# One scan of 448 columns in place of two of 224, in a state-space layer that runs beside DMA gathers

## The chip, the cores and the metric

The kernel runs on one core of a Trainium2 chip. The metric is the time of one execution on the device in microseconds. All times in the text are in us unless marked ns.

## What is computed

Four layers on eight images of 56 x 56 pixels with 128 channels. Layers 0, 2 and 3 are deformable convolutions with a feed-forward part behind them: for each pixel and each of 4 groups, 9 points with learned offsets are sampled from a table, weighted and added. Layer 1 is a state-space block (the scan), and this is its core:

```python
def step(h, t):
    dt_t, u_t, B_t, C_t = t
    h = h * jnp.exp(dt_t[..., None] * A) + (dt_t * u_t)[..., None] * B_t[:, :, None, :]
    y = jnp.einsum('bkdn,bkn->bkd', h, C_t)
    return (h, y)
ts = (dt.transpose(3, 0, 1, 2), xs.transpose(3, 0, 1, 2), Bsm.transpose(3, 0, 1, 2), Csm.transpose(3, 0, 1, 2))
h0 = jnp.zeros((B, K, Di, N), dtype=x.dtype)
_, ys = jax.lax.scan(step, h0, ts)
```

There are K = 4 directions over the image (by rows, by columns, and each of them backward), Di = 256 channels, N = 16 states and 3,136 pixels.

## The kernel before

**Work.** 24 stages (three convolution layers times eight images) follow one another; the state-space layer of each image runs beside them. In a stage, 24 tiles of 128 pixels and one of 64 are gathered: GpSimd issues one indirect DMA (L761) for every sampling point, 882 a stage, 21,168 in all, each of which reads its 128 indices from SBUF (`d_idx`). Twelve of them (six at the end of a stage) fill one of five buffers `d_g`. VectorE multiplies a buffer by its weights (L1369, "weigh"; the weights come from SBUF, or, where ScalarE has copied them, from PSUM, `l_pm`), PE adds it up through the identity (L1052, "sum"), and only then may GpSimd fill it again: it waits for the semaphore `accq` of the use five buffers earlier. Before every fourth tile it also waits for `idx`, the indices that VectorE computes in L1564.

**The scan.** The 256 channels are two halves of 128 partitions. An image is cut into 7 pieces of 448 pixels, times 4 directions, times 16 states: 448 steps an image, 3,584 in all. Step S needs for each half h the decay exp(dt*A) (ScalarE, L812), the product dt*u*B (VectorE, L1339, both halves in one instruction of 2 x 448 columns into the buffer `hb`, with B spread over the partitions by PE into the bank `l_pb`, L1003), the scan h = decay*h + product along the 448 pixels, in place in `hb`, and the product with C (VectorE, L1349, with C in the bank `l_pc`), which PE adds over the 16 states into `l_acc` (L1034). ScalarE saves the last column of both halves in `l_carry` (L793), from which the next piece's scan of that state begins.

The decay of half 0 lies in PSUM (`dA0`, a part of `l_pm`, one buffer), that of half 1 in SBUF (`dA1`, three buffers, shown as `l_wk`). `hb` has four buffers in SBUF, shown as `l_wk` too.

**Order.** A planner written in Python (class `Planner`) lays out one list of items for all engines before anything runs: ticks of the scan ("s", with PE's "sB" ahead of each), the weighing and summing of the gathers, and the pieces of the convolution, among them. Each engine walks through the list and issues its part of each item, with semaphores in between. The list doesn't depend on how long the instructions take. In a tick, VectorE's program (function `vector_program`) issues for step S: the scan of half 0 (L1326, 448 columns, semaphore `sh`), the first 224 columns of half 1 (L1328, semaphore `s1h`), the dt*u*B product of step S+1 (L1339, semaphore `f_pb`), after a wait for `s1h` (L1342) the other 224 columns of half 1 (L1343, semaphore `sh`), which start from the last column of the first part, and the C product of step S-1 (L1349, semaphore `f_pc`, with a wait for the carry, `ca`, L1348). For the directions 2 and 3 all goes backward along the columns.

**Who waits for a scan.** ScalarE's decay of half 0 for step S+1 waits for the scan of half 0 of step S (L809), since they share one buffer; its decay of half 1 for the step three later, and the carry (L792), wait for both halves. PE's spread of B for step S+2 waits for the product of step S+1 (`f_pb`), and its spread of C for the C product before it (`f_pc`).

Of the kernel before, what the change touches and what calls it, by code (L numbers as in the profile page):

```python
# [10 lines left out]
ALU = mybir.AluOpType  # L11
# [27 lines left out]
NSTEP = 16 * len(PIECES)  # L39
# [1224 lines left out]
def vector_program(e, J):  # L1264
    m, s = J.m, J.s
# [29 lines left out]
    for item in J.plan:  # L1295
        kind = item[0]
        if kind == "s":
            _, i, sig = item
            S = NSTEP * i + sig
            if sig >= 18 and sig % 16 == 2:  # L1300
                j = sig // 16 - 1
                P = 28 * i + j
                kd, c = PIECES[j]
# [11 lines left out]
            if 0 <= sig < NSTEP:  # L1315
                kd, c = PIECES[sig // 16]
                n = sig % 16
                hb, dA1 = m.hb[S % 4], m.dA1[S % 3]
                ini = [0.0 if c == (6 if kd >= 2 else 0) else m.carry[:, h, n:n + 1] for h in range(2)]

                way, one, two, mid = slice(None), slice(0, 224), slice(224, 448), 223
                if kd >= 2:
                    way, one, two, mid = slice(None, None, -1), slice(447, 223, -1), slice(223, None, -1), 224
                e.wait_ge(s["f_pb"], J.free("B", S))
                e.wait_ge(s["dA0"], S + 1)
                e.tensor_tensor_scan(hb[:, 0, way], m.dA0[:, way], hb[:, 0, way], ini[0], ALU.mult, ALU.add).then_inc(s["sh"], 1)  # L1326
                e.wait_ge(s["dA1"], S + 1)
                e.tensor_tensor_scan(hb[:, 1, one], dA1[:, one], hb[:, 1, one], ini[1], ALU.mult, ALU.add).then_inc(s["s1h"], 1)  # L1328
            if sig + 1 < NSTEP:
                x = S + 1  # L1330
                P, n = divmod(x, 16)
# [2 lines left out]
                if sig == -1:  # L1334
                    e.wait_ge(s["p_pc"], J.full("pi2", 7 * i + 6))
                    for b, v_ in enumerate(both(7 * i + 6)):
# [1 line left out]
                e.wait_ge(s["p_pb"], J.full("B", x))  # L1338
                e.tensor_tensor(m.hb[x % 4][:, :, :], m.dtu[P % 2][:, :, :], bc(m.pb[:, 0:448], 1, 2),  # L1339
                                ALU.mult).then_inc(s["f_pb"], 1)  # L1340
            if 0 <= sig < NSTEP:
                e.wait_ge(s["s1h"], S + 1)  # L1342
                e.tensor_tensor_scan(hb[:, 1, two], dA1[:, two], hb[:, 1, two], hb[:, 1, mid:mid + 1],  # L1343
                                     ALU.mult, ALU.add).then_inc(s["sh"], 1)
            if 1 <= sig <= NSTEP:
                x = S - 1
                e.wait_ge(s["p_pc"], J.full("C", x))
# [23 lines left out]
        elif kind == "h":  # L1371
            _, i, j, st = item
            P = 28 * i + j
            kd, c = PIECES[j]
# [148 lines left out]
        elif kind == "pr":  # L1523
# [11 lines left out]
            two = lambda x: x.rearrange("p t (j a) -> p t j a", a=2)  # L1535
# [54 lines left out]
        elif kind == "ch":  # L1590
# [45 lines left out]
PLAIN = ("c_w l_w da xi0 xi1 tab0 tab1 hdo dg htc xr0 xr1 xo0 xo1 vx0 vx1 xn0 xn1 z0 z1 vr0 vr1 vo0 vo1 "  # L1636
         "p_r0 p_r1 p_pm p_pb p_pc f_r0 f_r1 f_pm f_pb f_pc f_a0 f_a1 pa aexp cst dv "
         "weighed accq ysa ytp yta idx wtr w0 pv py exd bst agg sqd x1r xor gbr dgr bsq bnr "
         "wps dA0 dA1 s1h sh ca accd d1 d2 hd0 md m2 lo ab ex uu qq s1 ln pag psq xir brd lag lsq xmr gsq gt gb tg").split()


def program(nc, a, out, n_img=8, layers=(0, 1, 2, 3)):
    with ExitStack() as ctx:
        ctx.enter_context(nc.allow_non_contiguous_dma("weights and constants, once a stage"))

        def sb(name, shape, dt=F32):
            return ctx.enter_context(nc.sbuf_tensor(name, shape, dt))

        def ps(name, shape):
            return ctx.enter_context(nc.psum_tensor(name, shape, F32))  # L1650

        def dram(name, shape):
            return nc.dram_tensor(name, shape, F32, kind="Internal").ap()

        sems = {n: ctx.enter_context(nc.semaphore("s_" + n)) for n in list(PLAIN) + GSEMS}
        nums = sorted(sems[n].num for n in PLAIN)
        assert nums == list(range(nums[0], nums[-1] + 1))
        order, plan = schedule(n_img)
        J = Job(n_img, order, plan, Mem(sb, ps, dram, n_img), sems, a, out)
        with nc.Block() as block:  # L1660
            block.sync(lambda e: sync_program(e, J))
            block.gpsimd(lambda e: gpsimd_program(e, J))
            block.scalar(lambda e: scalar_program(e, J))
            block.vector(lambda e: vector_program(e, J))
            block.tensor(lambda e: tensor_program(e, J))
        totals = gather_totals(J)
        for q in range(0, len(totals), 10):
            part = totals[q:q + 10]
            nc.gpsimd.inc_swdge_sem([sems[g] for g, _ in part], [x for _, x in part], mode="sub")
        nc.all_engine_barrier(sems_to_clear=range(nums[0], nums[-1] + 1))  # L1670
# [75 lines left out]
```

## Time and profile before

| | |
|---|---|
| median of 3 runs | 29,863.57 us (29,856.42 to 29,863.9) |
| profiled execution, its time | 29,810.02 us |
| its span in the trace | 29,808.1 us |
| granted TensorE clock, mean | 0.848 of full speed |
| busy: PE | 22,658.6 us (76% of the span) |
| busy: VectorE | 22,829.2 us (77%) |
| busy: ScalarE | 12,217.9 us (41%) |
| busy: GpSimd | 21,878.7 us (73%) |
| mean DMA rate | 62 GB/s |

Engines are named PE (matmul), PEld (its weight loads), DVE (VectorE), ACT (ScalarE), POOL (GpSimd) and SP in the rows. In a group of instructions, `x` is the count, then come the busy time in us and the mean of one in ns, then the idle time of the engine just before them in us and what ended most of it. In the list of waits the columns are: who waited for whom, us in total, times, the longest. "issue" is time in which the engine waited for nothing that the profile shows; issuing itself doesn't count as busy, so GpSimd's 73% leaves out the time between two gathers. In a timeline the first number is the start in us, the second the duration in us, and the brackets hold the idle time of the engine before it, where there is any. Instructions of VectorE overlap a little in the records: the next one starts before the one ahead has written its last column.

### The profile page before, as it was taken

How to read it: one execution, taken by the hardware profiler on the slowest of the kernel's cores; microseconds unless marked ns; L12 is line 12 of the kernel's file. 1: busy time of each engine (PE TensorE's matmuls, PEld its weight loads, DVE VectorE, ACT ScalarE, POOL GpSimd, SP SyncE). 2: the span in 40 equal slices, each digit the busy share in tenths (PEclk: the TensorE clock that was granted, in tenths of full speed). 3: DMA queues.
4: the chain of work that ended last, by engine and by line, in shares of the span. 5: the costliest groups of instructions: out<-in, count | busy, mean ns of one | idle time of the engine just before them, and what ended most of it. 6: DMA issues, size and time to landing. Idle time of an engine off the chain costs nothing.

```text
span 29808.1 us, 287351 instructions
## 1 busy us (share of the span) xinstructions
PE 22658.6 (76%) x94224; PEld 14342.0 (48%) x94224; DVE 22829.2 (77%) x36118; ACT 12217.9 (41%) x21747; POOL 21878.7 (73%) x21172
## 2 busy tenths in 40 slices
PE   5588788787877888777878788777877787777444
PEld 4444455454544455444544454445544454445433
DVE  2398988989689879897799959986899869884212
ACT  1144444444444445444444444444444444443000
POOL 5777777777677777777677767776677767576767
PEclk7798888888888889888888888888988888887666
DMA  3212122221221222212222122212222121112221
GB/s 77 70 58 68 52 76 64 60 68 54 72 62 57 65 70 64 64 54 66 62 65 68 52 74 58 61 54 70 62 60 62 56 72 54 47 50 68 63 58 53
DMA packets 2410662, 1854.55 MB, mean 62 GB/s; under 512 B 1686546, under 2 KB 2045508, under 8 KB 2409164
## 3 DMA queue, kind: packets, MB, share of 16 engines
q0 software_dynamic: 677376, 1388.62, 15.4%
q1 hardware_dynamic: 1731788, 447.55, 6.7%
q8 instruction: 745, 12.21, 0.2%
q14 instruction: 753, 6.17, 0.1%
HBM read 1569.35 MB, written 265.21 MB: 62 GB/s over the span
## 4 chain that ended last, share of the span: by engine, by line
DVE 32%; PE 28%; POOL 17%; issue 13%; ACT 6%; DMA 1%; SPq 1%; DVEq 0%; ACTq 0%; POOLq 0%
POOL d_g L761 17%; DVE l_wk L1349 7%; DVE l_wk L1326 6%; PE d_p L1052 6%; PE l_acc L1034 5%; DVE l_wk L1343 5%; DVE d_g L1369 4%; PE d_pr L1200 3%; DVE l_wk L1328 2%; PE d_pr L1254 2%; ACT l_pm L812 2%; PE d_pr L1087 2%; PE d_pr L1066 1%; ACT L988 1%; PE d_pr L1247 1%
## 5 line engine op out<-in xcount | busy, mean ns | idle before, releaser
L761 POOL DMA_INDIRECT d_g<-table,d_idx x21168 | 21878.5, 1034 | 7886.6 <-issue 6402.6
L1034 PE MATMUL l_acc<-l_wk,c_ident 128*128 128x448 f32 x14336 | 7285.4, 638 | 384.9 <-DVE l_yx L1314 298.5
L1052 PE MATMUL d_p<-d_g,c_ident 128*128 128x128 f32 x43200 | 6013.0, 303 | 1955.5 <-DVE d_g L1369 1952.8
L1052 PEld LDWEIGHTS d_p<-d_g,c_ident 128*128 128x128 f32 x43200 | 5877.4, 218 | 3015.6 <-DVE d_g L1369 2067.6
L1339 DVE TENSOR_TENSOR l_wk<-l_wk,l_pb 128x896 f32<-128x896 f32 x3584 | 3816.9, 1065 | 1581.6 <-PE l_pb L1003 1577.0
L812 ACT ACTIVATE l_pm<-l_wk,l_a 128x448 f32<-128x448 f32 x3584 | 2270.9, 634 | 6219.4 <-DVE l_wk L1326 6203.8
L1034 PEld LDWEIGHTS l_acc<-l_wk,c_ident 128*128 128x128 f32 x14336 | 3171.3, 223 | 2453.9 <-issue 2276.4
L1349 DVE TENSOR_TENSOR l_wk<-l_wk,l_pc 128x896 f32<-128x896 f32 x3584 | 3795.7, 1059 | 20.7 <-ACT l_carry L793 16.5
L1326 DVE TENSOR_TENSOR_SCAN l_wk<-l_pm,l_carry,l_wk 128x448 f32<-128x448 f32 x3072 | 3498.6, 1139 | 4.9 <-ACT l_pm L812 2.6
L1369 DVE TENSOR_TENSOR d_g<-d_g,d_wt 128x512 f32<-128x512 f32 (+1 forms) x1248 | 798.0, 692 | 2204.3 <-DMA d_g<-table,d_idx 2204.1
L1343 DVE TENSOR_TENSOR_SCAN l_wk<-l_wk 128x224 f32<-128x224 f32 x3584 | 2422.1, 676 | 0.3
L1369 DVE TENSOR_TENSOR d_g<-d_g,l_pm 128x1536 f32<-128x1536 f32 (+1 forms) x1358 | 2350.0, 1730 | 60.5 <-DMA d_g<-table,d_idx 43.9
L812 ACT ACTIVATE l_wk<-l_wk,l_a 128x448 f32<-128x448 f32 x3584 | 2359.4, 659 | 15.1 <-DVE l_wk L1401 0.9
L1003 PE MATMUL l_pc<-l_spl,c_sel 96*128 96x448 bf16 x3584 | 1420.9, 396 | 1141.9 <-DVE l_wk L1349 1137.3
L1328 DVE TENSOR_TENSOR_SCAN l_wk<-l_wk,l_carry 128x224 f32<-128x224 f32 x3072 | 2017.5, 657 | 0.0
L1003 PE MATMUL l_pb<-l_spl,c_sel 96*128 96x448 bf16 x3584 | 1402.8, 391 | 634.1 <-DVE l_wk L1339 632.2
L793 ACT ACTIVATE l_carry<-l_wk 128x2 f32<-128x2 f32 x3584 | 722.8, 202 | 2593.9 <-DVE l_wk L1343 2588.3
L812 ACT ACT_TABLE_LOAD x1193 | 1530.6, 1283 | 20.9
L1200 PE MATMUL d_pr<-d_xt,d_diag 128*128 128x448 f32 x3024 | 1369.9, 597 | 34.1 <-ACT d_xt L927 27.1
L1003 PEld LDWEIGHTS l_pc<-l_spl,c_sel 96*128 96x128 bf16 x3584 | 369.8, 103 | 1836.7 <-DVE l_wk L1349 1677.1
L1254 PE MATMUL d_pr<-d_fc,d_ht 128*128 128x128 f32 (+1 forms) x4800 | 869.3, 337 | 502.3 <-ACT d_ht L988 502.1
L1247 PE MATMUL d_pr<-d_yt,d_fc 128*128 128x256 f32 (+1 forms) x2496 | 749.5, 428 | 540.3 <-ACT d_ht L988 454.3
(180 smaller groups left out, 23375.1 us busy)
## 6 DMA issues: line engine op xcount, KB each, us to landing
d_g<-table,d_idx POOLq DMA_INDIRECT x21168
table<-d_pst SPq DMA_DIRECT2D x2376, 64.0 KB
hd<-d_hst SPq DMA_DIRECT2D x168, 224.0 KB
d_htc<-hd SPq DMA_DIRECT2D x144, 256.0 KB
d_xin<-mid SPq DMA_DIRECT2D x112, 224.0 KB, 3.1
mid<-d_xo SPq DMA_DIRECT2D x192, 128.0 KB, 1.9
d_xres<-mid SPq DMA_DIRECT2D x192, 128.0 KB, 2.1
d_xin<-in_x SPq DMA_DIRECT2D x56, 224.0 KB, 3.4
```

Source lines behind the costliest of these rows:

```text
L761: e.indirect_dma_start(out=m.g[Q % SLOTS][:, j, :], out_offset=None, in_=m.table[k % 2], in_offset=bass.IndirectOffsetOnAxis(ap=m.idx[G % ...
L812: e.activation(m.dA0 if h == 0 else m.dA1[x % 3], m.dt[P % 2][:, h, :], ACT.Exp, scale=m.aa[:, kd, h, n:n + 1]).then_inc(s[f"dA{h}"], 1)
L1003: return e.matmul(bank[:, 0:448], m.sel[:, row + n:row + n + 1].to_broadcast([96, 128]), m.spl[P % 2][:, :], start=True, stop=True)
L1034: ins = e.matmul(m.acc[:, h, 0:448], m.ident[:, :], m.hb[x % 4][:, h, :], start=(n == 0), stop=(n == 15))
L1052: ins = e.matmul(m.p0[:, t % 2 * 128:t % 2 * 128 + 32 * w], m.ident[:, :], m.g[Q % SLOTS][:, w * p:w * p + w, 32 * r:32 * r + 32], start=( ...
L1200: ins = e.matmul(m.r[1][:, 0:448], m.diag[:, j, :], m.xt[:, 8 * c + dy:8 * c + dy + 8, dx:dx + 56], start=(j == 0), stop=(j == 8))
L1326: e.tensor_tensor_scan(hb[:, 0, way], m.dA0[:, way], hb[:, 0, way], ini[0], ALU.mult, ALU.add).then_inc(s["sh"], 1)
L1328: e.tensor_tensor_scan(hb[:, 1, one], dA1[:, one], hb[:, 1, one], ini[1], ALU.mult, ALU.add).then_inc(s["s1h"], 1)
L1339: e.tensor_tensor(m.hb[x % 4][:, :, :], m.dtu[P % 2][:, :, :], bc(m.pb[:, 0:448], 1, 2), ALU.mult).then_inc(s["f_pb"], 1)
L1343: e.tensor_tensor_scan(hb[:, 1, two], dA1[:, two], hb[:, 1, two], hb[:, 1, mid:mid + 1], ALU.mult, ALU.add).then_inc(s["sh"], 1)
L1349: e.tensor_tensor(m.hb[x % 4][:, :, :], m.hb[x % 4][:, :, :], bc(m.pc[:, 0:448], 1, 2), ALU.mult).then_inc(s["f_pc"], 1)
L1369: ins = e.tensor_tensor(g, g, wt, ALU.mult)
```

## The change

The scan of half 1 becomes one instruction of 448 columns, directly behind the scan of half 0 and ahead of the dt*u*B product of the next step; it starts from the carry, as its first part did. The second part, the wait for `s1h` and that semaphore are gone. Nothing else is changed; `sh` still counts two for each step.

```diff
-                way, one, two, mid = slice(None), slice(0, 224), slice(224, 448), 223
-                if kd >= 2:
-                    way, one, two, mid = slice(None, None, -1), slice(447, 223, -1), slice(223, None, -1), 224
+                way = slice(None, None, -1 if kd >= 2 else None)
                 e.wait_ge(s["f_pb"], J.free("B", S))
                 e.wait_ge(s["dA0"], S + 1)
                 e.tensor_tensor_scan(hb[:, 0, way], m.dA0[:, way], hb[:, 0, way], ini[0], ALU.mult, ALU.add).then_inc(s["sh"], 1)
                 e.wait_ge(s["dA1"], S + 1)
-                e.tensor_tensor_scan(hb[:, 1, one], dA1[:, one], hb[:, 1, one], ini[1], ALU.mult, ALU.add).then_inc(s["s1h"], 1)
+                e.tensor_tensor_scan(hb[:, 1, way], dA1[:, way], hb[:, 1, way], ini[1], ALU.mult, ALU.add).then_inc(s["sh"], 1)
...
                 e.tensor_tensor(m.hb[x % 4][:, :, :], m.dtu[P % 2][:, :, :], bc(m.pb[:, 0:448], 1, 2),
                                 ALU.mult).then_inc(s["f_pb"], 1)
-            if 0 <= sig < NSTEP:
-                e.wait_ge(s["s1h"], S + 1)
-                e.tensor_tensor_scan(hb[:, 1, two], dA1[:, two], hb[:, 1, two], hb[:, 1, mid:mid + 1],
-                                     ALU.mult, ALU.add).then_inc(s["sh"], 1)
```

## Rows read from the trace of the kernel before

**Rows 1.** List of waits, whole span: waiter, releaser: us, times, longest

```profile
POOL d_g L761 <- DVE d_idx L1564: 886.6, 11, 303.7
POOL d_g L761 <- PE d_p L1052: 597.5, 148, 34.3
...
DVE l_wk L1339 <- PE l_pb L1003: 1577.0, 739, 10.8
```

**Rows 2.** The gathers: their group, then duration ns min/median/max, first and last start

```profile
L761 POOL DMA_INDIRECT d_g<-table,d_idx x21168 | 21878.5, 1034 | 7886.6 <-issue 6402.6
...
L761 POOL DMA_INDIRECT d_g<-table,d_idx x21168: 938/944/3096, 159.3 to 29764.6; - x200
```

**Rows 3.** Groups, stretch 27,449 to 28,554 us (first), then 2,454 to 3,642 us

```profile
L761 POOL DMA_INDIRECT d_g<-table,d_idx x882 | 836.7, 949 | 359.5 <-issue 268.5 <-DVE d_idx L1564 91.0
...
L761 POOL DMA_INDIRECT d_g<-table,d_idx x882 | 919.9, 1043 | 268.8 <-issue 268.5 <-PE d_p L1052 0.3
...
L1343 DVE TENSOR_TENSOR_SCAN l_wk<-l_wk 128x224 f32<-128x224 f32 x186 | 125.7, 676 | 0.0
```

**Rows 4.** Waits: DVE, 1,400 to 13,406 us (first); POOL, 1,395 to 27,029 us

```profile
DVE d_g L1369 <- DMA d_g<-table,d_idx: 40.1, 15, 8.0
...
POOL d_g L761 <- PE d_p L1052: 573.8, 145, 34.3
POOL d_g L761 <- DVE d_idx L1564: 530.7, 8, 303.7
```

**Rows 5.** Timeline of DVE and POOL from 12,019 us

```profile
12019.36 0.68 DVE L1343 TENSOR_TENSOR_SCAN l_wk<-l_wk 128x224 f32<-128x224 f32 x1
12019.53 1.26 POOL L761 DMA_INDIRECT d_g<-table,d_idx  x1 [0.30 <-issue]
...
12021.10 1.12 DVE L1326 TENSOR_TENSOR_SCAN l_wk<-l_pm,l_carry,l_wk 128x448 f32<-128x448 f32 x1
12021.10 0.94 POOL L761 DMA_INDIRECT d_g<-table,d_idx  x1 [0.30 <-issue]
...
12022.13 0.66 DVE L1328 TENSOR_TENSOR_SCAN l_wk<-l_wk,l_carry 128x224 f32<-128x224 f32 x1
12022.34 1.20 POOL L761 DMA_INDIRECT d_g<-table,d_idx  x1 [0.30 <-issue]
```

**Rows 6.** Timeline of DVE and POOL from 12,069 us

```profile
12069.69 1.81 DVE L1407 TENSOR_TENSOR l_wk<-l_wk,l_xb 128x896 f32<-128x896 f32 x1
12069.99 2.33 POOL L761 DMA_INDIRECT d_g<-table,d_idx  x1 [0.30 <-issue]
```

**Rows 7.** Timeline of DVE alone, one tick without other work

```profile
11999.58 0.65 DVE L1328 TENSOR_TENSOR_SCAN l_wk<-l_wk,l_carry 128x224 f32<-128x224 f32 x1
12000.15 1.05 DVE L1339 TENSOR_TENSOR l_wk<-l_wk,l_pb 128x896 f32<-128x896 f32 x1
12001.13 0.67 DVE L1343 TENSOR_TENSOR_SCAN l_wk<-l_wk 128x224 f32<-128x224 f32 x1
12001.73 1.05 DVE L1349 TENSOR_TENSOR l_wk<-l_wk,l_pc 128x896 f32<-128x896 f32 x1
12002.71 1.13 DVE L1326 TENSOR_TENSOR_SCAN l_wk<-l_pm,l_carry,l_wk 128x448 f32<-128x448 f32 x1
12003.77 0.65 DVE L1328 TENSOR_TENSOR_SCAN l_wk<-l_wk,l_carry 128x224 f32<-128x224 f32 x1
```

**Rows 8.** Lines L1328 and L1343: duration ns min/median/max, first and last start

```profile
L1328 DVE TENSOR_TENSOR_SCAN l_wk<-l_wk,l_carry x3072: 647/657/697, 1494.6 to 27028.2; 128x224 f32<-128x224 f32 x192
...
L1343 DVE TENSOR_TENSOR_SCAN l_wk<-l_wk x3584: 666/676/743, 1399.0 to 27028.9; 128x224 f32<-128x224 f32 x200
```

**Rows 9.** Costliest groups of the page: second half scan, B spread

```profile
L1343 DVE TENSOR_TENSOR_SCAN l_wk<-l_wk 128x224 f32<-128x224 f32 x3584 | 2422.1, 676 | 0.3
...
L1003 PE MATMUL l_pb<-l_spl,c_sel 96*128 96x448 bf16 x3584 | 1402.8, 391 | 634.1 <-DVE l_wk L1339 632.2
```

**Rows 10.** Timeline of POOL at the start of a stage

```profile
3671.72 0.94 POOL L761 DMA_INDIRECT d_g<-table,d_idx  x1 [29.21 <-DVE d_idx L1564]
```

More of the change, by code:

```diff
@@ L1638 @@
          "weighed accq ysa ytp yta idx wtr w0 pv py exd bst agg sqd x1r xor gbr dgr bsq bnr "
-         "wps dA0 dA1 s1h sh ca accd d1 d2 hd0 md m2 lo ab ex uu qq s1 ln pag psq xir brd lag lsq xmr gsq gt gb tg").split()
+         "wps dA0 dA1 sh ca accd d1 d2 hd0 md m2 lo ab ex uu qq s1 ln pag psq xir brd lag lsq xmr gsq gt gb tg").split()
 def program(nc, a, out, n_img=8, layers=(0, 1, 2, 3)):
```

## The prediction, on record before the result was known

> **What bounds the kernel now.** I began with the page's busy times of the engines. PE, VectorE and GpSimd lie close together and none is near the whole span, so the shares name no bound. The list of waits does [rows 1]: in a span of 29,808 us GpSimd waits 886.6 us for the indices and 597.5 us for PE to give a gather buffer back, and for nothing else. The rest of its time is gathers, 21,168 of them at a mean of 1,034 ns, with 6,402.6 us of its own issue between them, 0.30 us each [rows 2]. 21.88 + 6.40 + 0.89 + 0.60 ms is 29.77 of 29.81 ms: the chain of gathers is the span, and nothing can be gained that doesn't shorten it.
>
> Next: what sets the length of a gather. Its median is 944 ns, its shortest 938, its longest 3,096 [rows 2]. The difference of mean and median, 90 ns, times 21,168 is 1.9 ms of stall inside gathers. In a stage without scans (27,449 to 28,554 us) the mean is 949 ns, in one of the same 882 gathers with 186 scan steps (2,454 to 3,642 us) 1,043 ns [rows 3]. So the stall comes with the scan steps: 94 ns x 882 = 83 us a stage.
>
> VectorE doesn't wait for gathers there: in the first half of the stretch with scans it waited 40.1 us for them, while over the whole stretch GpSimd waited 573.8 us for buffers and 530.7 us for indices [rows 4], 303.7 of this in one wait [rows 1]. Gathers, and the VectorE and PE work interleaved with them, go at nearly one pace, with the five buffers between.
>
> **What stalls a gather.** In the timeline [rows 5] the gather begun at 12,019.53 took 1.26 us. The second half scan (L1343) ran until 12,020.04 and the gather ended at 12,020.79, 0.75 us behind it. The gather of 12,022.34 took 1.20 us, and ended 0.75 us after the first half scan (L1328) had. Between them the scan L1326, whose decay lies in PSUM, covered a whole gather, which took 0.94. A gather thus needs something about 0.19 us after its start (0.94 - 0.75), and where a VectorE instruction with both operands in SBUF is running then, it waits for the end of that instruction. A long one holds it to its end too: the product L1407, 1.81 us, stretched a gather to 2.33 us, which ended 0.82 us behind it [rows 6].
>
> The Trainium skill ("SBUF — State Buffer", section "SBUF: two separate sides") has this as a lock on a port pair that the two engines share, held for the whole instruction, by VectorE also with two SBUF inputs against a GpSimd operation that reads SBUF. It speaks against the change, which makes one long hold of two short ones. By the same rule the scans should wait for gathers as well; in the trace they don't.
>
> **The parts, priced.**
>
> 1. VectorE time. In a tick without other work [rows 7] the starts are 0.57 us apart from L1328 to the next instruction, 0.60 from L1343 to the next, 1.06 for the PSUM scan of 448 columns, and 4.19 us from one L1328 to the next. The trace has no SBUF scan of 448 columns. From above its price is the sum of the two, 1.17 us (no gain); from below it is 1.00, the PSUM scan's 1.06 less twice the 0.03 by which the two half scans differ, the only spread of scans in these rows. I take 1.04, near the PSUM scan of the same length. So each step saves 0.13 us, 3,584 steps [rows 8] 0.47 ms of VectorE time. It isn't on the chain of gathers, so it counts only as below.
>
> 2. The wait removed, L1342, costs 0.3 us of idle time before all L1343 together [rows 9]: nothing. What covered it, the product, now stands behind the scan. The product of step S+1 comes about 0.47 us later in the tick, and PE gets the bank of B so much later; behind it PE waits for the C product anyway, 0.98 us later in the tick, which is longer than the B matmul, 0.39 us [rows 9]. Nothing, and if that cover were gone 0.47 us a step at most, on PE. In the other direction the 1,577.0 us in which the product waited for B [rows 1] shrink, since a whole scan comes first. ScalarE's carry is released about 1.1 us earlier in the tick; VectorE needs it only in the next tick.
>
> 3. Gather stalls. A gather comes to this point once in 0.94 + 0.30 = 1.25 us. If an instruction that holds it, of length L, falls there at a random phase, it is hit with chance L/1.25 and costs L/2 on the mean: L x L/2.5 us. Two half scans: (0.57² + 0.60²)/2.5 = 0.274 us a step. A control: 186 steps of it are 51 of the 83 us found above, and the rest is left for the other SBUF operations (L1407 and its neighbours), which is plausible. One scan of 1.04: 0.433 us. The difference is +0.159 us a step, x 3,584 = **+0.57 ms**. Lower bound: in ticks without other work the phases lock. After a stalled gather the next ones ask 1.25, 2.49 and 3.74 us after the scan's end, the next scan runs from 3.04 to 4.08, so each costs 0.34 us: 1.22 ms against 0.98, +0.24 ms. Upper bound: all 1.9 ms of stall belongs to the scans and grows by 0.433/0.274 = 1.58: +1.1 ms. I take +0.57: most steps are longer than the clean tick (25.6 ms over 3,584 steps is 7.15 us against 4.19), so phases are mixed.
>
> 4. What GpSimd gets back. In a stage VectorE's side becomes 186 x 0.13 = 24 us shorter and GpSimd's 186 x 0.159 = 30 us longer. So VectorE, now up to some tens of us behind the gathers, catches up. Short waits for indices such as the 29.21 us at the start of the stage at 3,671.72 [rows 10] should mostly go: 530.7 - 303.7 = 227 us there are, I take half, 115. Of the 573.8 us for buffers I take a fifth, 115, since they fall where the scans rest between two images and PE is busy with other work, and only the delay carried into them shrinks. Together -0.23 ms; at least 0, at most 0.8.
>
> Sum: 0.57 - 0.23 = +0.34 ms. The profiled execution took 29,810.0 us, so 30,150; the median of the runs, 29,863.6, lies 54 us above it, so I forecast **30,205 us** (+1.1%).
>
> **Rivals.**
>
> A. The stall without the return: VectorE's lead changes no wait of GpSimd, because PE is what is late where GpSimd waits. For: those waits are for PE's L1052. Against: the waits for indices end on VectorE. 29,864 + 570 = 30,430 us.
>
> B. Pace of VectorE (faster). If a long scan let a gather through before its end, or if phase locking kept the new stall at its lower bound or less, the 0.47 ms saved and part of the 1.58 ms of waiting for B would pull the indices and the buffers forward. GpSimd can get back no more than 227 + 574 us; I take 500 of them, against 240 of stall: 29,600 us. It decides where the added stall is below what comes back, thus below some 0.07 us a step. Against it: the timeline [rows 5, 6], in which each stalled gather waits to the end of the instruction.
>
> C. Cancelling: stall near the lower bound (+0.24) and return as above (-0.23): 29,870 us, no change.
>
> D. A gather that held VectorE up in turn would make one scan better than two (one wait instead of two). The half scans lasted 647 to 697 and 666 to 743 ns [rows 8]: never stretched by a gather's length. By the skill's rule, whoever starts first blocks the other, this would be worth up to 0.3 us a step and would end on the fast side; I count it within B.
>
> **Numbers.** The forecast, with its neighbourhood of +0.15 to +0.50 ms, 0.62; A, with +0.50 to +0.75, 0.20; C 0.10; B with D 0.08. 0.2% (60 us) is about what a measurement of this kernel can tell from no change. The range reaches from just above C to past A: 29,950 to 30,490. Slower by over 0.2%: 0.83; within: 0.09; faster: 0.08.
>
> **What would show it.** Gathers: median still 944, mean near 1,061 (570 us/21,168 = +27 ns), fewer gathers stretched but each by more, up to about 1.0 us. A new row of 3,584 scans of 448 columns from SBUF at about 1,120 ns, each stalled gather ending 0.75 us after one. VectorE's busy time lower by about 0.4 ms, its wait for gathers between 1,395 and 27,029 us up from tens to hundreds of us, its wait for B lower; GpSimd's waits for indices and buffers each some 100 us lower. A mean gather at or below 1,040 ns would make the forecast wrong at step 3; an unchanged 1,484 us of waits of GpSimd would make it wrong at step 4, and A right.

## The result: 0.3% faster, where 1.1% slower was forecast

The changed kernel took 29,773.5 us (median of 7 runs) against 29,856.6 us (7 runs) of the kernel before: ratio 0.9971, 95% interval 0.9959 to 0.9982. Run again later beside other kernels, it took 29,716.6 against 29,833.1 us, 0.9964 (0.9950 to 0.9978). Small, but clear of noise, and of the other sign than the forecast.

The profile after. First the page's engines and two of its groups, the gathers and the new scan (columns as in [rows 2]):

```profile
PE 22695.4 (76%) x94224; PEld 14377.9 (48%) x94224; DVE 22442.9 (75%) x32534; ACT 12184.7 (41%) x21747; POOL 22097.4 (74%) x21172
...
L761 POOL DMA_INDIRECT d_g<-table,d_idx x21168 | 22097.2, 1044 | 7636.4 <-issue 6424.4
...
L1337 DVE TENSOR_TENSOR l_wk<-l_wk,l_pb 128x896 f32<-128x896 f32 x3584 | 3831.1, 1069 | 1401.1 <-PE l_pb L1003 1389.9
...
L1326 DVE TENSOR_TENSOR_SCAN l_wk<-l_wk,l_carry 128x448 f32<-128x448 f32 x3072 | 3468.6, 1129 | 0.0
```

Then the list of waits over the whole span, against [rows 1], and GpSimd's over 1,395 to 27,029 us and VectorE's for gathers over 1,400 to 13,406 us, against [rows 4]:

```profile
DVE d_g L1363 <- DMA d_g<-table,d_idx: 2731.1, 446, 14.3
...
DVE l_wk L1337 <- PE l_pb L1003: 1389.9, 635, 10.0
...
POOL d_g L761 <- DVE d_idx L1558: 793.4, 9, 297.6
```

```profile
POOL d_g L761 <- DVE d_idx L1558: 438.3, 6, 297.6
POOL d_g L761 <- PE d_p L1052: 393.3, 86, 23.4
...
DVE d_g L1363 <- DMA d_g<-table,d_idx: 244.4, 98, 13.1
```

GpSimd's time still adds up to the span. Its gathers became 218.7 us longer, its issue 21.8; its wait for indices fell by 93.2 and its wait for buffers (597.5 to 418.4) by 179.1: -31.8 us in all, and the span fell by 31.5. In this one execution the median gather was 947 ns instead of 944, which is 64 of the 218.7 us; in the second execution of the same kernel it was 944 again:

```profile
L761 POOL DMA_INDIRECT d_g<-table,d_idx x21168 | 22035.2, 1041 | 7636.5 <-issue 6418.4 <-DVE d_idx L1558 785.5 <-PE d_p L1052 432.6
```

There it is +156.7 and +15.8 against -101.1 and -164.9, -93.5 us, and the span is 93.5 us below that of before. This one is used below. So what GpSimd got back, 266 us, is near what step 4 of the prediction had (230). What its gathers lost is a quarter of what step 3 had: 157 us instead of 570.

**Where the stall went.** For each gather over 15 ns longer than the median I took the excess, and put it down to a scan where the VectorE instruction that ended some 0.75 us before the gather's end was one, and to other instructions where it wasn't (behind most of those the gather ends 0.82 us later, not 0.75). Before: scans 0.80 ms, others 1.10 ms, together 1.90. Changed: scans 1.25, others 0.81, together 2.06. The scans rose by 0.45 ms, near the forecast; the *others*, which the change doesn't touch, fell by 0.29 ms. That is the question for the experiments.

### The profile page after: what moved, and what is told of

Read it like the earlier page. It is cut to its first block, busy times and chain, and to the rows that moved or that the text cites. A ratio compares the mean times of both kernels' runs of the same rounds, so it can differ in the third digit from the quotient of the medians.

```text
span 29776.6 us, 283767 instructions
## 1 busy us (share of the span) xinstructions
PE 22695.4 (76%) x94224; PEld 14377.9 (48%) x94224; DVE 22442.9 (75%) x32534; ACT 12184.7 (41%) x21747; POOL 22097.4 (74%) x21172
## 4 chain that ended last, share of the span: by engine, by line
POOL 54%; issue 18%; PE 14%; DVE 10%; ACT 2%; DMA 1%; SPq 1%; DVEq 0%; POOLq 0%; ACTq 0%
POOL d_g L761 54%; PE d_p L1052 3%; PE l_acc L1034 2%; PE d_pr L1200 2%; DVE l_wk L1343 2%; DVE l_wk L1324 2%; DVE l_wk L1337 1%; DVE l_wk L1326 1%; DVE d_g L1363 1%; PE d_pr L1087 1%; PE d_pr L1254 1%; PE l_pc L1165 1%; SPq L660 1%; DMA d_xin<-mid 0%; PE d_pr L1066 0%
## 5 line engine op out<-in xcount | busy, mean ns | idle before, releaser
L761 POOL DMA_INDIRECT d_g<-table,d_idx x21168 | 22097.2, 1044 | 7636.4 <-issue 6424.4
L1052 PE MATMUL d_p<-d_g,c_ident 128*128 128x128 f32 x43200 | 6075.5, 305 | 2236.0 <-DVE d_g L1363 2233.0
L1343 DVE TENSOR_TENSOR l_wk<-l_wk,l_pc 128x896 f32<-128x896 f32 x3584 | 3878.0, 1082 | 22.5 <-ACT l_carry L793 19.4
L1326 DVE TENSOR_TENSOR_SCAN l_wk<-l_wk,l_carry 128x448 f32<-128x448 f32 x3072 | 3468.6, 1129 | 0.0
L1003 PEld LDWEIGHTS l_pb<-l_spl,c_sel 96*128 96x128 bf16 x3584 | 369.1, 103 | 1833.8 <-DVE l_wk L1337 1391.9
L1254 PEld LDWEIGHTS d_pr<-d_fc,d_ht 128*128 128x128 f32 (+1 forms) x4800 | 745.4, 235 | 702.2 <-ACT d_ht L988 643.7
L1604 DVE BATCH_NORM_STATS2 d_bs<-d_pr 128x6 f32<-128x128 f32 (+1 forms) x1200 | 296.7, 288 | 954.1 <-PE d_pr L1256 710.9
```

The costliest lines, as they stand in the source:

```text
L761: e.indirect_dma_start(out=m.g[Q % SLOTS][:, j, :], out_offset=None, in_=m.table[k % 2], in_offset=bass.IndirectOffsetOnAxis(ap=m.idx[G % ...
L1003: return e.matmul(bank[:, 0:448], m.sel[:, row + n:row + n + 1].to_broadcast([96, 128]), m.spl[P % 2][:, :], start=True, stop=True)
L1052: ins = e.matmul(m.p0[:, t % 2 * 128:t % 2 * 128 + 32 * w], m.ident[:, :], m.g[Q % SLOTS][:, w * p:w * p + w, 32 * r:32 * r + 32], start=( ...
L1254: e.matmul(bank[0:n, i * 128:i * 128 + 128], m.ht[:, f, i * n:i * n + n], m.fc2[:, f, :], start=(f == 0), stop=False)
L1326: e.tensor_tensor_scan(hb[:, 1, way], dA1[:, way], hb[:, 1, way], ini[1], ALU.mult, ALU.add).then_inc(s["sh"], 1)
L1343: e.tensor_tensor(m.hb[x % 4][:, :, :], m.hb[x % 4][:, :, :], bc(m.pc[:, 0:448], 1, 2), ALU.mult).then_inc(s["f_pc"], 1)
```

## The experiments

Theory SPACING: after a gather that a scan has stalled, the next ones ask at fixed times after the scan's end, and what they meet there depends on the order of VectorE's instructions. Theory AMOUNT: each instruction stalls gathers by its length, wherever it stands. The change has two parts, a merge and a move of the second half, and two kernels do one part each.

**Move alone** (first group, e1):

```diff
                 e.tensor_tensor_scan(hb[:, 1, one], dA1[:, one], hb[:, 1, one], ini[1], ALU.mult, ALU.add).then_inc(s["s1h"], 1)
+                e.wait_ge(s["s1h"], S + 1)
+                e.tensor_tensor_scan(hb[:, 1, two], dA1[:, two], hb[:, 1, two], hb[:, 1, mid:mid + 1],
+                                     ALU.mult, ALU.add).then_inc(s["sh"], 1)
             if sig + 1 < NSTEP:
...
-            if 0 <= sig < NSTEP:
-                e.wait_ge(s["s1h"], S + 1)
-                e.tensor_tensor_scan(hb[:, 1, two], dA1[:, two], hb[:, 1, two], hb[:, 1, mid:mid + 1],
-                                     ALU.mult, ALU.add).then_inc(s["sh"], 1)
```

> The two half scans stay two, but both stand ahead of the dt*u*B product, the second directly behind the first, as the one scan of the changed kernel does. Theory SPACING (what a gather loses depends on how far behind the scan the next instruction with two SBUF operands comes: a stalled gather's successors ask again 1.25 and 2.49 us after the scan's end, and this kernel puts two PSUM products of 0.98 us between): the other SBUF instructions cost as little as in the changed kernel, mean gather 1,040 to 1,050 ns, GpSimd's waits smaller than before, time 20 to 100 us below the kernel before. Theory AMOUNT (each instruction stalls gathers by its own length squared over 2.5 us, wherever it stands; the gain came from the shorter VectorE time): two short holds as before, VectorE no shorter, time within 30 us of the kernel before, mean gather 1,034 to 1,038 ns.

**Merge alone** (e2), from the changed kernel:

```diff
-                e.wait_ge(s["dA1"], S + 1)
-                e.tensor_tensor_scan(hb[:, 1, way], dA1[:, way], hb[:, 1, way], ini[1], ALU.mult, ALU.add).then_inc(s["sh"], 1)
             if sig + 1 < NSTEP:
...
+            if 0 <= sig < NSTEP:
+                e.wait_ge(s["dA1"], S + 1)
+                e.tensor_tensor_scan(hb[:, 1, way], dA1[:, way], hb[:, 1, way], ini[1], ALU.mult, ALU.add).then_inc(s["sh"], 1)
             if 1 <= sig <= NSTEP:
```

> One scan of 448 columns, but where the second half stood, between the two products. SPACING: a hold of 1.04 us, and other SBUF instructions still follow 0.98 us behind its end, where the next gather (1.25 us) falls into them: scans stall about 1.2 ms as in the changed kernel, the others stay at their 1.1 ms of before; mean gather 1,052 to 1,062 ns, time 50 to 250 us above the kernel before. AMOUNT: the same as the changed kernel, mean 1,044 ns and a time 50 to 110 us below before.

**No hold** (e3 from the changed kernel; e4 does the same to both half scans of the kernel before). Half 1 is scanned with half 0's decay, which lies in PSUM, so its own decay is left out of the result and no scan has both operands in SBUF:

```diff
                 if h == 0 and x:
-                    e.wait_ge(s["sh"], 2 * x - 1)
+                    e.wait_ge(s["sh"], 2 * x)
...
-                e.tensor_tensor_scan(hb[:, 1, way], dA1[:, way], hb[:, 1, way], ini[1], ALU.mult, ALU.add).then_inc(s["sh"], 1)
+                e.tensor_tensor_scan(hb[:, 1, way], m.dA0[:, way], hb[:, 1, way], ini[1], ALU.mult, ALU.add).then_inc(s["sh"], 1)
```

> The changed kernel with the scan of half 1 reading half 0's decay, which lies in PSUM, so that no scan has two SBUF operands (the result of half 1 is that of the other decay; ScalarE's next decay of half 0 waits for both scans). The lengths of VectorE's instructions stay. If the scans are what stalls the gathers, their 1.24 ms of stall goes: mean gather 975 to 1,000 ns. Both theories expect that. If gathers are then still the bound, the time falls by 0.8 to 1.1 ms; if VectorE and PE go at nearly the same pace, GpSimd's waits for buffers and indices rise by more than half of what is saved and the time falls by 0.1 to 0.5 ms. I expect the second.

> The kernel before with both half scans reading the decay in PSUM. Against the other kernel without holds it differs only in VectorE's order and in 0.13 us a step of VectorE time. Mean gather 975 to 1,000 ns, the same as there within 5 ns. If VectorE's time is the bound once the holds are gone, this kernel is 0.2 to 0.5 ms slower than the other; if not, they are equal within 60 us.

*Measured.* This group ran on another chip, on which the kernel before took 34,921 us. Ratios to it there: move 0.9976 (0.9962 to 0.9991), merge 0.9986 (0.9975 to 0.9997), no hold after 1.0022 (1.0007 to 1.0037), no hold before 1.0217 (1.0204 to 1.0231). The waits of the merged kernel there:

```profile
POOL d_g L761 <- PE d_p L1052: 3609.5, 510, 38.0
DVE l_wk L1335 <- remote: 3322.6, 499, 41.6
...
POOL d_g L761 <- DVE d_idx L1559: 1508.7, 23, 346.4
```

GpSimd waits 3.6 ms for buffers instead of 0.5, and VectorE 3.3 ms for a releaser that the profile finds on none of this core's engines. The gathers aren't the bound on that chip: taking 80 ns off each gather (1,051 to 971 ns) made nothing faster. What holds up PE and VectorE there wasn't tried. The group shows the stalls: mean gather 988 ns with the move, 1,051 with the merge, 971 and 973 without holds. Its times say nothing of this kernel's bound on the first chip, so move, merge and no hold were run again on one where the kernel before takes 29.83 ms, as at first. Several expectations missed here: the move's mean gather is far below the 1,040 to 1,050 ns that SPACING had, the merged kernel came out 50 us faster where SPACING had it slower, and e3 got slower where it should have gained. e4 has e3's mean gather within 5 ns, as expected, and is 686 us slower than e3, more than expected. Its edit has a side effect: ScalarE may write half 0's next decay only after the second half, late in the tick. ScalarE waited 9.9 ms for that scan (7.9 ms in e3), but VectorE only 8 us for the decay, so this wait isn't shown to be the cause; what makes the +2.2% stays open.

**The second group** has the changed kernel again (f1), merge alone (f2), move alone (f3), and the scan as the last of the tick (f4):

```diff
             if 0 <= sig < NSTEP:
...
-                e.wait_ge(s["dA1"], S + 1)
-                e.tensor_tensor_scan(hb[:, 1, way], dA1[:, way], hb[:, 1, way], ini[1], ALU.mult, ALU.add).then_inc(s["sh"], 1)
...
                                 ALU.mult).then_inc(s["f_pc"], 1)
+            if 0 <= sig < NSTEP:
+                e.wait_ge(s["dA1"], S + 1)
+                e.tensor_tensor_scan(hb[:, 1, way], dA1[:, way], hb[:, 1, way], ini[1], ALU.mult, ALU.add).then_inc(s["sh"], 1)
```

> The changed kernel once more, beside the others of this group. On a chip on which the kernel before takes 29.8 to 29.9 ms: ratio 0.996 to 0.998, mean gather 1,044 ns (both theories). On one like that of the last group (kernel before 34.9 ms, engines held up from outside for tens of us at a time, GpSimd waiting 3 to 4 ms for buffers): ratio 0.98 to 1.00, since there VectorE's time counts and the gathers' stall doesn't.

> One scan of 448 columns between the two products, as in the last group. SPACING, on a chip where the gathers are the bound: mean gather 1,052 to 1,062 ns, the scans stalling 1.2 ms and the others 1.1 ms; time 100 to 300 us above the changed kernel. AMOUNT: equal to the changed kernel within 40 us.

> Two half scans, both ahead of the product. In the last group this kernel had the lowest gather time of the four with holds (mean 988 ns, against 1,051 for the merged scan between the products), on a chip where gathers were not the bound. SPACING, where they are: mean gather 1,000 to 1,030 ns, time 150 to 400 us below the kernel before, below the changed kernel too: a gather gets in between the halves and the others follow two products later. AMOUNT: mean 1,034 to 1,040 ns, within 40 us of the kernel before.

> The scan of half 1 in one piece as the last instruction of the tick, behind both products, so that another instruction with two SBUF operands follows it at once, and a gather that waits for the scan waits for that one too. SPACING: no gather gets in between; the stalls add up, mean gather 1,055 to 1,080 ns, time 150 to 500 us above the changed kernel. AMOUNT: equal to the changed kernel within 60 us.

*Measured.* Ratios: merge alone 1.0105 (1.0088 to 1.0122), move alone 0.9983 (0.9973 to 0.9992), scan last 1.0006 (0.9996 to 1.0015), the changed kernel 0.9964. The gathers' groups, in the order f2, f3, f4:

```profile
L761 POOL DMA_INDIRECT d_g<-table,d_idx x21168 | 22407.8, 1059 | 7672.8 <-issue 6420.4 <-DVE d_idx L1559 791.2 <-PE d_p L1052 461.2
```

```profile
L761 POOL DMA_INDIRECT d_g<-table,d_idx x21168 | 20988.6, 992 | 8743.1 <-issue 6369.2 <-DVE d_idx L1563 1389.8 <-PE d_p L1052 983.7
```

```profile
L761 POOL DMA_INDIRECT d_g<-table,d_idx x21168 | 21606.2, 1021 | 8195.0 <-issue 6393.5 <-DVE d_idx L1559 1145.7 <-PE d_p L1052 655.8
```

AMOUNT falls: f2 has the changed kernel's instructions in another order and is 418 us slower. GpSimd's terms say where: against f1 its gathers are 373 us longer, its waits and issue 36, and the span is 409 us longer. The merge where the half stood costs about what the prediction said of the whole change (+302 us, ratio 1.0105, against +340 forecast). Merge and move don't add: at the new place the merge takes 59 us off (29,776 to 29,717), at the old one it adds 302. SPACING's numbers missed in part too: f2 is further above the changed kernel than the 100 to 300 us expected, and f3 has a mean gather of 992 ns (1,000 to 1,030 expected) but is only 57 us below the kernel before, not 150 to 400, and not below the changed kernel.

The timelines show why. Merge alone:

```profile
1741.30 1.15 DVE L1339 TENSOR_TENSOR_SCAN l_wk<-l_wk,l_carry 128x448 f32<-128x448 f32 x1
1741.67 1.53 POOL L761 DMA_INDIRECT d_g<-table,d_idx  x1 [0.30 <-issue]
1742.36 1.06 DVE L1344 TENSOR_TENSOR l_wk<-l_wk,l_pc 128x896 f32<-128x896 f32 x1
1743.34 1.08 DVE L1388 SCALAR_TENSOR_TENSOR l_wk<-l_wk 128x896 f32<-128x896 f32 x1
1743.51 1.74 POOL L761 DMA_INDIRECT d_g<-table,d_idx  x1 [0.30 <-issue]
```

The changed kernel (f1), at a similar place:

```profile
1830.91 1.12 DVE L1326 TENSOR_TENSOR_SCAN l_wk<-l_wk,l_carry 128x448 f32<-128x448 f32 x1
1831.05 1.73 POOL L761 DMA_INDIRECT d_g<-table,d_idx  x1 [0.31 <-issue]
1831.95 1.06 DVE L1337 TENSOR_TENSOR l_wk<-l_wk,l_pb 128x896 f32<-128x896 f32 x1
1832.93 1.08 DVE L1343 TENSOR_TENSOR l_wk<-l_wk,l_pc 128x896 f32<-128x896 f32 x1
1833.09 0.94 POOL L761 DMA_INDIRECT d_g<-table,d_idx  x1 [0.30 <-issue]
1833.93 1.08 DVE L1387 SCALAR_TENSOR_TENSOR l_wk<-l_wk 128x896 f32<-128x896 f32 x1
1834.34 1.49 POOL L761 DMA_INDIRECT d_g<-table,d_idx  x1 [0.30 <-issue]
```

A stalled gather ends 0.75 us after the scan; the next starts 0.30 later and needs VectorE's operands out of the way 0.19 after that: 1.24 us behind the scan's end, whatever the phase was before, and then at 2.49 and 3.74. In the first timeline one PSUM product stands between scan and the next SBUF instruction, which therefore runs from 0.89 to 1.97 us behind: it is met early, and the gather takes 1.74. In the second there are two products, it runs from 1.90 to 2.98, the gather at 1.24 goes free and the one at 2.49 takes 1.49: 0.55 us lost instead of 0.80. The kernel before had the first spacing. There, a stalled first half also led to a stalled second half, 0.9 to 1.6 us behind it; that is why two adjacent halves (f3) stall 0.48 ms in all, against 0.80 before.

The whole traces bear this out. For each gather stalled by a scan I counted whether one of the next three was stalled by another instruction (gathers that follow without a wait, none stalled between):

| kernel | stalled by a scan | next one met | second | third |
|---|---|---|---|---|
| before (halves) | 3,108 | 920, 0.53 ms | 21 | 32, 0.02 ms |
| merge alone (f2) | 2,548 | 1,347, 0.74 ms | 18 | 0 |
| changed (f1) | 2,511 | 4 | 910, 0.39 ms | 91, 0.03 ms |
| scan first (g2, below) | 2,428 | 0 | 1 | 516, 0.20 ms |

The gather that is met is the one that the timelines name, in each kernel. Of the 0.35 ms by which the others' stall differs between f2 and f1, 0.33 lies here. Between the kernel before and f1 it is 0.13 of the 0.29 ms; the rest lies with gathers further from a scan and wasn't traced to its cause. In the kernel before, 1,035 of the 1,369 gathers stalled by a first half were followed by one stalled by the second half, 0.34 ms; in f3 none was. The others fell lower in f3 than in f1, which SPACING had not expected, and its own arithmetic gives the reason: the second half ends 0.72 us after the first, so gathers behind a stalled first half ask 0.52, 1.77 and 3.01 us behind the second, and the instruction that runs from 1.89 to 2.97 falls between. The second gather was met in 53 of 1,205 cases behind a stalled first half (0.01 ms), and in 409 of 984 behind a stalled second half (0.19 ms).

The expectation for f4 was wrong. I had said that a gather waiting for the scan would wait for the SBUF instruction behind it too:

```profile
1732.19 1.15 DVE L1345 TENSOR_TENSOR_SCAN l_wk<-l_wk,l_carry 128x448 f32<-128x448 f32 x1
1732.75 1.34 POOL L761 DMA_INDIRECT d_g<-table,d_idx  x1 [0.30 <-issue]
1733.25 1.07 DVE L1388 SCALAR_TENSOR_TENSOR l_wk<-l_wk 128x896 f32<-128x896 f32 x1
...
1734.39 0.96 POOL L761 DMA_INDIRECT d_g<-table,d_idx  x1 [0.31 <-issue]
```

It gets in at the scan's end, 0.75 us before its own, and the instruction behind is over when the next asks. The others' stall is 0.42 ms, and the time is 131 us above the changed kernel, not 150 to 500. That kernel still isn't fast: VectorE now comes to the B product 1.06 us into its tick and waits 2.0 ms for PE's B, and GpSimd's waits rise to 1.80 ms:

```profile
DVE l_wk L1335 <- PE l_pb L1003: 2019.3, 914, 9.1
```

**The third group.** The C product ahead, the scan last (g1); the scan of half 1 first (g2, ScalarE's wait as in e3); no hold (g3, the same edit as e3); both decays in SBUF (g4). The diff is g4's; its second part makes ScalarE wait, at the start of an image, until that stretch of SBUF is free:

```diff
-        self.dA0, self.dA1 = self.pm[:, 0:448], [wk[5][:, 0, :], wk[5][:, 1, :], wk[6][:, 0, :]]
+        self.dA0, self.dA1 = wk[6][:, 1, :], [wk[5][:, 0, :], wk[5][:, 1, :], wk[6][:, 0, :]]
...
-                if h == 1 and q == 0 and i:
+                if q == 0 and i:
                     e.wait_ge(s["p_pc"], J.full("mo", 7 * i - 1))
```

> The order is scan of half 0, C product, B product, whole scan of half 1. In the last group the scan as the last instruction had a mean gather of 1,021 ns, lower than the changed kernel's 1,041 and not higher as SPACING had said: a gather gets in at the scan's end, and the SBUF instruction that follows is over or nearly so when the next asks, 1.25 us later. What that kernel lost was on VectorE, which came to the B product 1.06 us into the tick and waited 2,019 us for PE's B. Here the B product comes 2.04 us in, as in the changed kernel. SPACING, so corrected: mean gather 1,015 to 1,025 ns, wait for B 1,300 to 1,600 us, time 100 to 350 us below the kernel before, the fastest of all. AMOUNT (all merged kernels alike): equal to the changed kernel within 50 us, mean 1,041.

> The order is whole scan of half 1, scan of half 0, B product, C product; ScalarE's next decay of half 0 waits for both scans, 1.04 us earlier in the tick than two scans end. Other SBUF instructions come 3.0 us behind the hold; gathers ask again at 1.25, 2.49 and 3.74. SPACING: an instruction of 1.0 us that starts 3.0 us behind is hit at 3.74 and stalls 0.3 us, less than the 0.49 of the changed kernel: mean gather 1,030 to 1,040 ns, time 0 to 150 us below the changed kernel. AMOUNT: equal to it.

> The changed kernel with no scan that has two SBUF operands (half 1 scans with half 0's decay, from PSUM), as in the first group, now on a chip where gathers are the bound. Mean gather 965 to 985 ns (there 971). VectorE's instructions keep their lengths. By the kernel with two halves ahead of the product (mean 992 ns, but GpSimd waiting 2.4 ms for buffers and indices instead of 1.2) I expect that VectorE and PE are then the bound: GpSimd's waits 2.2 to 2.6 ms, time 100 to 400 us below the changed kernel. If gathers alone bound it, it would be 1.2 ms below.

> The changed kernel with the decay of half 0 in SBUF too, so that both scans hold: 2.1 us in one stretch with, at most, a short opening between. If a gather gets in between them (as behind the last scan in the last group): stalls rise by another 0.3 to 0.8 ms, mean gather 1,055 to 1,080 ns. If it doesn't: a hold of 2.1 us, each of the 3,584 met once, 1.0 us on the mean: 3.6 ms in place of 1.25, mean gather 1,150 ns. In both cases the gathers are the bound and the time rises by what they lose: +0.3 to +0.8 ms, or +2.3 ms.

*Measured.* Ratios: g1 1.0091 (1.0074 to 1.0108), g2 0.9926 (0.9910 to 0.9943), g3 0.9890 (0.9874 to 0.9907), g4 1.0127 (1.0110 to 1.0143). All kernels of the two later groups (kernel before 29,833 and 29,831 us in them), with the stalls added up as above (ms), GpSimd's two waits (ms) and the median time:

| kernel | stall by scans | by others | mean gather, ns | waits | us |
|---|---|---|---|---|---|
| before | 0.80 | 1.10 | 1,034 | 1.48 | 29,833 |
| changed (f1) | 1.25 | 0.81 | 1,041 | 1.22 | 29,717 |
| merge alone (f2) | 1.26 | 1.16 | 1,059 | 1.25 | 30,135 |
| move alone (f3) | 0.48 | 0.53 | 992 | 2.37 | 29,776 |
| scan last (f4) | 1.20 | 0.42 | 1,021 | 1.80 | 29,847 |
| C, B, scan (g1) | 1.24 | 0.42 | 1,022 | 2.06 | 30,105 |
| scan first (g2) | 1.07 | 0.54 | 1,020 | 1.56 | 29,605 |
| no hold (g3) | 0 | 0.65 | 974 | 2.53 | 29,507 |
| both in SBUF (g4) | 1.87 | 0.69 | 1,065 | 1.21 | 30,205 |

The stall in g1 is as expected, the time isn't (+274 us, where 100 to 350 us less was expected): the C product now comes first, and VectorE waits for the C that PE spreads only after the C product before it:

```profile
DVE l_wk L1329 <- PE l_pc L1003: 1987.5, 857, 9.7
```

g2 beats both kernels, the one before by 0.74% and the changed one, with its 0.9964 in its own group, by 0.4%, as expected; its mean gather of 1,020 ns is below the 1,030 to 1,040 expected. Its other SBUF instructions run from 2.93 us behind the scan's end and are met at 3.74:

```profile
1532.23 1.15 DVE L1324 TENSOR_TENSOR_SCAN l_wk<-l_wk,l_carry 128x448 f32<-128x448 f32 x1
1532.85 1.28 POOL L761 DMA_INDIRECT d_g<-table,d_idx  x1 [0.30 <-issue]
...
1536.31 1.09 DVE L1387 SCALAR_TENSOR_TENSOR l_wk<-l_wk 128x896 f32<-128x896 f32 x1
1536.92 1.29 POOL L761 DMA_INDIRECT d_g<-table,d_idx  x1 [0.30 <-issue]
```

That gather loses 0.35 us to the other instruction, against 0.55 in the changed kernel and 0.80 with one product between.

g3 gives the worth of the scans' holds and the second bound; its gathers:

```profile
L761 POOL DMA_INDIRECT d_g<-table,d_idx x21168 | 20622.8, 974 | 8886.1 <-issue 6356.8 <-DVE d_idx L1558 1344.3 <-PE d_p L1052 1185.0
```

Without any hold of a scan, 1.41 ms of stall go against the changed kernel and 0.21 ms of time; GpSimd's waits take 1.31 ms back. g4 doubles the held time and adds only 0.50 ms of stall, with a time 488 us above the changed kernel's: a gather that waits for the first scan gets in ahead of the second, and asks again when that is over. g3 and g4 came out within all that was expected of them.

## Why the prediction was wrong, point by point

- *What bounds the kernel.* Right: the changes of GpSimd's four terms add up to the change of the span within 0.3 us. But "nothing can be gained that doesn't shorten it" hid that VectorE and PE stand right behind: f3 and g3, in which gathers lose 0.9 and 1.25 ms less than before, gain 0.2 and 1.1%. Their waits of 2.4 to 2.5 ms are the other chain's.
- *Step 1.* Right: the scan took 1,129 ns, the next instruction started 1.04 us after it in most ticks, and VectorE's busy time fell by 386 us.
- *The step that failed: the stall of the other instructions, in step 3, put at no change without a reason.* The whole stall was to grow by 0.57 ms and grew by 0.16. The scans' own term was near: +0.45 ms. But the instructions that the control in step 3 called "the rest" hold 1.10 of the 1.90 ms, and they lost 0.29. The prediction saw that phases lock from tick to tick, used that for a lower bound of the scans alone, and never asked it of the others: the control left 32 us a stage to them, and no term asked where they stood.
- *Step 2, where that entered.* It priced the move at "nothing", by PE's and ScalarE's waits alone. The wait for B did shrink (1,577 to 1,390 us). But the move also changes what stands between two instructions with SBUF operands: with the merged scan this is worth 418 us (f2 to f1, which differ by the move alone), with two halves 57 (f3).
- *Sizes in step 3.* The sum by random phases stood too high on both sides, measured were a fifth less: 0.80 ms for 0.98 before, 1.25 for 1.55 after. The lower bound set a locked 1.22 ms, which was nearly what was measured, against that unlocked 0.98; and by [rows 7] the next scan runs from 3.02 us, not 3.04. The sign that was to show step 3 wrong, a mean gather at or below 1,040 ns, lay too low: the mean was 1,044 and 1,041, with the stall at a quarter of the forecast.
- *Step 4.* Near in size: 266 us came back, where 230 were taken, and the waits for indices and for buffers fell by 101 and 165 us. Rival A falls. VectorE's wait for gathers rose from 40 to 244 us in the first half, the sign that it caught up. The merge without the move (f2) brought back 232 us. How much of this is owed to the shorter scans, and how much to the slower gathers, which leave GpSimd less to wait for, no run separates.
- *The rivals.* C had the place right, stall and return cancelling, but got there by a small stall of the scans, which wasn't so. B had the sign, and one of its two conditions held: the new stall stayed under the lower bound of 0.24 ms, by locked phases. But the scans' part didn't; the other instructions' phases brought it there, which B did not name, and 266 us came back, not 500. Its other condition, a gather let through before the scan's end, is refuted by each timeline here. D falls: the whole scans last 1,052 to 1,185 ns in f1, none stretched by a gather's length.
- *The rule.* That a gather waits to the end of the instruction, as the Trainium skill has it ("SBUF — State Buffer", section "SBUF: two separate sides"), agrees with all timelines. Its other half, that VectorE waits where the gather was first, shows in none of them. Put into the prediction's steps 3 and 4 it priced the merge at the old place to within 40 us, and the whole change with the wrong sign.

The range (29,950 to 30,490) would have held f2, not the change made.

## What to carry to other kernels

Where two engines contend for something at a near-fixed period, the order of the instructions that hold it matters as much as their length: write down when the stalled one asks again (here 1.24, 2.49, 3.74 us) and what runs then. Count the stalls by the instruction that ends just before the release, over all instructions and not the edited ones alone. And where a second chain is a fraction of a per cent behind the first, no larger saving on the first counts in full; one run with the contention in question taken out (g3, the scans' holds) shows what there is to gain from it, here 1.1%.

## What was not expected of the hardware

A gather waiting on a VectorE instruction gets in between it and the next one that would hold it, even where the two overlap by 0.05 to 0.1 us in the records (f4: 0.08 us). This holds behind other instructions than scans too: in the kernel before, 109 stalled gathers ended 0.82 us behind a weighing from SBUF (L1369) whose successor, another weighing from SBUF, had begun 0.08 us before its end. A wider count fits with it. A gather reaches the point at which it can be held 0.19 us after its start; in f1, of 419 that reached it in the first 0.2 us of a whole scan, 390 went free, and all 2,079 that reached it later than 0.3 us after the scan's start and earlier than 0.15 us before its end were held. So a hold is some 0.2 us shorter than the scan in the records, which may be why step 3's sums for the scans stood too high; no run shows what makes the first 0.2 us free.

And the same program took 17% longer on another chip, with engines idle for tens of us at a time and no releaser among them, and there the merge and the move each changed the time by 0.1 to 0.2% only.
